# Top-64 attention: GpSimd lowers the scores below the 64th largest, ScalarE then takes exponentials and sums in place

## The reference, cut to what matters

```python
q, k = l2norm(q), l2norm(k)                        # k and v begin with 4 memory rows
dots = einsum('bhid,bhjd->bhij', q, k) * 10
dots = einsum('hg,bgij->bhij', W_pre_th, dots)     # heads are mixed
dots = where(causal, mask_value, dots)
# of each row only the 64 largest scores are kept
attn = softmax(dots)
attn = einsum('hg,bgij->bhij', W_post_th, attn)    # heads are mixed again
```

## Time and profile before

| | us |
|---|---|
| median of 3 runs | 4011.19 (4008.38 to 4012.89) |
| span of the profiled execution | 4014.9 |
| PE busy | 3618.5 (90%) |
| DVE busy | 3649.1 (91%) |
| ACT busy | 3158.1 (79%) |
| POOL busy | 723.3 (18%) |

### The profile page before, as it was taken

The page is one execution under the profiler, slowest core; times in us unless marked ns, Lnnn a source line. Parts: engine busy times, 40 slices in busy tenths (PEclk is TensorE's granted clock), DMA queues, the critical chain, the costliest instruction groups (busy, mean ns, idle before and its releaser), DMA issues. The chain is left out here.

```text
span 4014.9 us, 78409 instructions
## 1 busy us (share of the span) xinstructions
PE 3618.5 (90%) x19551; PEld 2620.4 (65%) x19551; DVE 3649.1 (91%) x19949; ACT 3158.1 (79%) x10004; POOL 723.3 (18%) x2487
## 2 busy tenths in 40 slices
PE   4999999986899999999999998999999999999987
PEld 3888888873566666666666666666666666666655
DVE  6888888845999999999999999999999999999995
ACT  5777777755788888888888888888888888888863
POOL 0000000002222222222222222222222222222221
PEclk8999999996999999999999999999999999999999
DMA  3000000001111111111111111111111111111110
GB/s 120 11 11 12 11 12 11 9 9 34 27 26 27 31 31 30 32 27 27 28 27 27 27 26 27 30 29 27 26 29 31 32 32 27 27 28 26 25 25 4
DMA packets 168119, 105.96 MB, mean 26 GB/s; under 512 B 78000, under 2 KB 165104, under 8 KB 166896
## 3 DMA queue, kind: packets, MB, share of 16 engines
q1 hardware_dynamic: 167664, 100.96, 11.8%
HBM read 20.70 MB, written 8.91 MB: 7 GB/s over the span
## 5 line engine op out<-in xcount | busy, mean ns | idle before, releaser
L1698 DVE MAX8 last<-W 128x8 f32<-128x130 f32 (+17 forms) x4032 | 944.2, 274 | 0.0
L1680 DVE MATCH_REPLACE8 W<-last,W 128x130 f32<-128x130 f32 (+17 forms) x3456 | 873.3, 259 | 0.0
L884 DVE TENSOR_TENSOR_SCAN hs<-dA,dx 128x256 f32<-128x256 f32 x512 | 351.2, 686 | 135.8 <-issue 100.7
L1789 POOL TENSOR_SCALAR posts<-post,share 128x128 f32<-128x128 f32 x1024 | 367.0, 376 | 513.0 <-DVE share L1612 510.1
L1487 ACT ACTIVATE SN<-bank,rq 128x260 f32<-128x260 f32 (+1 forms) x1024 | 361.3, 431 | 90.4 <-PE bank L1297 74.2
L1312 PE MATMUL bank<-T,pre 128*128 128x40 f32 (+15 forms) x1024 | 368.1, 442 | 62.5 <-DMA T<-SN 37.1
L1322 PE MATMUL bank<-posts,T 128*128 128x128 f32 (+7 forms) x2048 | 385.2, 291 | 3.6 <-POOL posts L1789 2.8
L1297 PE MATMUL bank<-kT,qT 64*128 64x260 f32 (+1 forms) x2048 | 275.1, 373 | 116.0 <-ACT SN L1487 108.3
L1322 PEld LDWEIGHTS bank<-posts,T 128*128 128x128 f32 (+7 forms) x2048 | 279.7, 170 | 94.3 <-issue 54.5
L1474 ACT ACTIVATE E<-T,peak 128x260 f32<-128x260 f32 (+12 forms) x800 | 305.3, 432 | 2.9
L1312 PEld LDWEIGHTS bank<-T,pre 128*128 128x128 f32 x1024 | 168.3, 195 | 206.4 <-ACT T L1495 95.2
(11 more groups left out here) (243 smaller groups left out, 8775.4 us busy)
## 6 DMA issues: line engine op xcount, KB each, us to landing
T<-SN SPq DMA_DIRECT2D x32, 130.0 KB
x_in<-in_xT SPq DMA_DIRECT2D x32, 128.0 KB, 2.3
x_mid<-x_b SPq DMA_DIRECT2D x32, 128.0 KB, 1.7
xb<-x_mid SPq DMA_DIRECT2D x32, 128.0 KB, 2.1
out_y<-x_d SPq DMA_DIRECT2D x32, 128.0 KB, 3.4
T<-SN SPq DMA_DIRECT2D x32, 126.0 KB
T<-SN SPq DMA_DIRECT2D x32, 122.0 KB
T<-SN SPq DMA_DIRECT2D x32, 118.0 KB
```

The costliest lines, as they stand in the source:

```text
L884: dve.tensor_tensor_scan(hs[j % NH][:], dA[j % ND][:], dx[b % 2][:], 0.0, ALU.mult, ALU.add).then_inc(scanned, 1)
L1680: dve.match_replace(both[:, s, at:to], best[n], both[:, s, at:to], LOWEST).then_inc(ranked, 1)
L1698: dve.max(best[n], both[:, s, at:to]).then_inc(ranked, 1)
L1789: pool.tensor_scalar(posts[(4 * k + j) % NP][:], post[:], share[k % 2][:, j:j + 1], 1.0, ALU.mult, ALU.mult).then_inc(posts_made, 1)
```

## The change

- `keep` and the tiles `E` are gone from DVE and ACT. DVE's rank ends with the MAX8 that finds the threshold; it raises `found_wide` or `found_narrow`.
- New on POOL: `drop(b, i)`, once for each quad. For each pair of groups that has something to cut (13 pairs in a block) it writes, group by group, -1e30 or 0 into the tile `below` (TENSOR_SCALAR, is_lt or is_gt with the threshold, then mult; a memset for group 6) and then adds the pair's `below` to the scores in `T` (TENSOR_TENSOR).
- ACT takes all 32 exponentials of a block in place in `T`, with the sum. It now waits for `dropped` (or, for whole pairs, for the mask).
- DVE's `rank` of quad k waits at its start for `dropped` of quad k-2 and `peaked` of quad k-2; for low groups that are not wide the TENSOR_REDUCE comes first. `turn_over` no longer waits for DVE's cuts; the new waits ahead of `wide` and `narrow` are on DVE's own earlier steps.
- ACT's table switches are made by `table(name)`, which loads a set only if another one is loaded; the `ACT_SET` beats are gone.
- All beats are new. DVE's rank still fills beats 16i to 16i+15.

```diff
-    E = [room.sb(f"E{j}", [P, KEYS if j < 2 else W_LO]) for j in range(4)]
+    below = [room.sb(f"below{n}", [P, 2 * (KEYS, W_LO)[n]]) for n in range(2)]
...
-    ACT_PEAK = (-2, 1, 34, 48, 64, 70, 81, 103)
-    ACT_WIDE = (-1, 20, 37, 50, 66, 70, 85, 103)
-    ACT_NARROW = (12, 30, 38, 50, 67, 73, 86, 114)
-    ACT_SET = (41, 52, 68, 79)
-    ACT_GATES = (47, 48, 50, 51)
-    ACT_SILU = (60, 61)
-    ACT_H1 = (70, 70)
-    ACT_H2 = (73, 74)
-    DVE_SHARE = (36, 38, 50, 65, 89, 98, 120, 130)
+    ACT_PEAK = (7, 10, 18, 52, 56, 63, 116, 131)
+    ACT_WIDE = (10, 12, 27, 54, 66, 83, 122, 131)
+    ACT_NARROW = (11, 17, 31, 56, 67, 102, 122, 131)
+    ACT_GATES = (31, 34, 43, 47)
+    ACT_SILU = (39, 41)
+    ACT_H1 = (60, 62)
+    ACT_H2 = (67, 75)
+    DVE_SHARE = (40, 51, 69, 85, 111, 111, 122, 136)
+    POOL_SHARE = (22, 30, 33, 47, 74, 87, 91, 121)
+    POOL_DROP = (-1, 21, 27, 30, 51, 61, 72, 101)
...
         def exps(b, i, pair):
             k = QUADS * b + i
+            table(EXP_LN)
             act.wait_ge(peaked, k + 1)
+            if k >= 4:
+                act.wait_ge(shared, k - 3)
+            if 2 * pair in DROPS[i]:
+                act.wait_ge(dropped, drops(k, 2 * pair))
+            else:
+                act.wait_ge(masked, HALF * b + PAIR_AT[QUAD[i][2 * pair]] + 1)
             for j in (2 * pair, 2 * pair + 1):
...
-                    act.activation(E[j][:, 0:n], scores(b, g), ACT.Exp, bias=least).then_inc(e_made, 1)
+                one = scores(b, QUAD[i][j])
+                act.activation(one, one, ACT.Exp, bias=peak[k % 2][:, j:j + 1], accum_out=total[k % 4][:, j:j + 1]).then_inc(e_made, 1)
...
-        def keep(b, i, j, best, base, op):
-
-            k, g = QUADS * b + i, QUAD[i][j]
-            dve.wait_ge(e_made, 4 * k + j + 1)
-            dve.scalar_tensor_tensor(out=scores(b, g), in0=base, scalar=best, in1=E[j][:, 0:width(g)], op0=op, op1=ALU.mult,
-                                     accum_out=total[k % 4][:, j:j + 1]).then_inc(cut_made, 1)
...
+        def drop(b, i):
+
+            nonlocal marks
+            k, made = QUADS * b + i, []
+            for j0 in DROPS[i]:
+                g = QUAD[i][j0]
+                w, x = width(g), side_by_side(b, g)
+                out = below[j0 // 2][:, 0:2 * w].rearrange("p (two n) -> p two n", two=2)
+                if drops(k, j0) > 1:
+                    pool.wait_ge(dropped, drops(k, DROPS[i][0]) - 1)
+                if g in WIDE:
+                    pool.wait_ge(found_wide, 2 * ((QUADS + 1) * b + i + j0 // 2 + 1))
+                else:
+                    pool.wait_ge(found_narrow, len(TURNED) * b + 1 + TURNED.index(QUAD[i][j0 + 1]))
+                for j in (j0, j0 + 1):
+                    one, best = QUAD[i][j], last8[k % 2][:, j, :]
+                    s, at = side(one), (seen_by(one) - TOPK) % 8
+                    if one in WIDE:
+                        pool.tensor_scalar(out[:, s, :], x[:, s, :], best[:, 7:8], DROP, ALU.is_lt, ALU.mult).then_inc(marked, 1)
+                    elif one in TURNED:
+                        pool.tensor_scalar(out[:, s, :], neg[2 * (i % 2) + one % 2][:, 0:w], best[:, at:at + 1], DROP, ALU.is_gt,
+                                           ALU.mult).then_inc(marked, 1)
+                    else:
+                        pool.memset(out[:, s, :], 0.0).then_inc(marked, 1)
+                marks += 2
+                made.append((x, out, marks))
+            for x, out, n in made:
+                pool.wait_ge(marked, n)
+                pool.tensor_tensor(x, x, out, ALU.add).then_inc(dropped, 1)
```

235 lines of the change are left out of this document (121 added, 114 removed).

## The result

The changed kernel takes 4057.51 us (median of 4 runs, 4057.01 to 4059.75) against 4012.04 for the kernel before on the same chip: the recorded ratio is 1.0104, with a 95% interval of 1.0092 to 1.0116 (the two medians alone give 1.0113). It is 1.0% slower. The prediction was 3876, faster, with a range up to 4030: wrong in sign and by 181 us.

What follows compares the result with a forecast made beforehand. DVE was taken to set the pace, PE next. Both at 86.5 us plus 3.5 of gaps gave 90.0 a block against 94.3: 138 us less over 32 blocks, 3 more in the drain, 3876 median; range 3800 to 4030.

Steps and rivals of the forecast that it cites:

- DVE, what is removed: Removing `keep` takes 8.8 us a block of busy time off DVE, from 92.3 to 83.5.
- I price them at nothing: DVE's new waits on its own earlier steps cost nothing, a few tenths of a us at most.
- POOL, what is added: The drops add 21 us a block on POOL, 10.3 compares and 10.6 adds; POOL goes from 22 to 43.
- the compare at the two-input slope, 26 us: Upper bound for POOL's added work a block, pricing compares by TENSOR_TENSOR's 1.9 ns a column.
- 0.4 to spare: Quad 7's chain from drop to share takes 4.6 us and fits in about 5 us of the next rank.
- The place of the drop: Behind quad 7's rank, the drop takes 3.0 us and four exponentials 1.6 before the share in the next block.
- ACT: Added accumulator reads cost up to 2.5 us a block, fewer table loads save 6.4: from 79.5 to about 75.6.
- The shared port: DVE's two-input operations lose 3.0 us a block beside POOL, between 0 and 11, putting DVE at 86.5.
- slower: the port: Rival: 18 opening TENSOR_TENSORs of DVE each wait a whole POOL instruction; 96.5 us a block, 4085 us; chance 0.14.
- PE: PE's work is unchanged, only its order changes: 86.5 us a block.
- The sum: DVE and PE both need 86.5 us; with 3.5 allowed for gaps, 90.0 a block, 4.3 less, over 32 blocks.
- The chain behind `drop` is late: Rival: late drops make DVE or PE wait, losing two to four us a block; 3947 to 4003 us; chance 0.19.

Runs made afterwards that it cites:

- the subtraction's run: The changed kernel with POOL's compare replaced by a subtraction, then a multiplication by 0, so nothing is dropped: 4042.6 us.
- filling: The changed kernel with matmuls of constants, result overwritten, in TensorE's gaps ahead of the first norm's spread and two premixes: 3996.5 us.
- the second version: Changed kernel with quads 6, 7 marked on DVE, quad 7's adds ahead of the mask, quad 4's posts ahead of drop 6: 4002.9 us; gaps filled, 3942.2.

## Why the prediction was wrong

Point by point, by its own steps.

- **DVE, what is removed.** Near: 85.0 us a block (forecast 83.5, with the port 86.5), by two errors that nearly cancel. `keep` gave 7.4 us and not 8.8, since its start and end run under its neighbours: the trace before, with L1618 taken out, is busy 84.9 us a block. The port cost 0.1 to 0.2 in place of 3.0. The step "I price them at nothing", of DVE's waits on its own steps, held; a new one on POOL's adds (L1728) takes 0.4 us a block.
- **POOL, what is added.** This is the step that failed: "25 x 0.27 + 4196 x 0.00083 = 10.3 us". It is 23.4. The slope was taken from multiplications; 21.2 of the 23.4 us are the compares with nothing of DVE's beside them, 2.2 what they lose beside DVE. The adds were right. The stated upper bound, "the compare at the two-input slope, 26 us", was one for compares and adds together (it makes the 48 of "29 to 48"), and it didn't hold either: the drops take 34.6 us and POOL 57.5. No row before the change had a compare on POOL, so neither of the two slopes was a bound. Nor was it carried on what even 26 would do to "0.4 to spare" for quad 7.
- **The place of the drop.** "For quad 7 it takes 3.0 us" was 5.3, and the drop began 2.9 us after the rank's end, behind the mask on POOL: 4.6 us of chain became 9.4. The queue was read for what stands behind the drops, not for what stands ahead.
- **ACT.** Right: 75.7 us, and 192 table loads, 6 a block.
- **The shared port.** DVE paid next to nothing; POOL did, by 0.39 to 0.50 us for each compare that starts beside the opening of a rank. The 0.11 us a piece was read from L1659 beside `neg` against L1688, another step; in the changed kernel L1674 of 180 columns, with nothing of POOL's beside it, takes 338, which leaves 0.08. The rival "slower: the port" gave the right sign by a mechanism that did not occur.
- **PE.** "86.5 us a block" was 87.4. The work was the same; the clock was lower. Missing from the prediction is that a gap of PE can cost twice, once as a wait and again as slower matmuls behind it; its clock was put at "0.99" for both kernels without a term.
- **The sum.** "I allow 3.5" for waits between two full engines; PE idles 8.4 us a block and DVE 10.9. Near the forecast's price of a drop (24.1 us a block for 21) and with the clock nearly held the kernel takes 3917.7, 1.3 us a block more than 3876: that is what the allowance missed. So, of the 181 us, 97 are the compare's price, 15 are those of the subtraction's run, of open cause, 28 are the clock at the low price, and 42 are left, by difference, for waits. The shares hang on the order in which they are taken: at the real price the clock alone is worth 61.
- **The rivals.** "The chain behind `drop` is late" was the right mechanism, mis-sized: 2 to 4 us a block lost were thought of, 5.8 came (95.8 - 90.0), the lower clock in it, and it was not let across the line to slower.

The Trainium skill ("SBUF — State Buffer", section "Who interferes with whom") has the shared port pair as an exclusive lock, held by whoever issues first. The trace agrees in part: POOL's instruction that starts beside DVE's pair loses time (0.8 us where 0.3 is usual at 2 columns), but DVE's L1701 of 180 columns, which starts under a running compare, takes 337 ns, as L1674 of that width does with nothing beside it (338), so it waits for no lock.

The Trainium skill ("TensorE: Matmul & The Clock Gate", section "HAM oscillation — how this bites in real kernels") charges a throttled stretch at half its length. By that the 5.3 us a block that filling took away (5.9 to 0.6) would be worth 2.7, an estimate of 85 us over 32 blocks; filling gave 61 here, and in the second version, where 10.1 us a block went, it gave 61 again for an estimate of 162, so the rule is an upper figure for this case.

What stays open: why the subtraction was 15 us faster than the compare at nearly the same price; how the 61 us of the filling divide between the spread and the premixes, which were filled together; and which waits make up the last 42 us.

## What to carry to other kernels

Price an instruction by rows with the same operation, not only with the same engine, width and operands: on POOL a compare of 180 columns took 0.89 us and a multiplication 0.41. A slope of another operation is no upper bound: here it said 26 us and 34.6 came. When a step goes on an in-order engine, look at what stands ahead of it too, and carry a price that no row shows through the tightest chain before giving the sign. When a change opens gaps on TensorE, count them as lost clock as well; a few matmuls of constants ahead of a known wait gave 1.5% here, about as much as moving marks to DVE and mending POOL's order together (1.3%).

## What the runs showed of the hardware

- POOL's TENSOR_SCALAR, with nothing of DVE's ranks beside it: at 132 columns 730 ns for is_lt against a per-partition operand and a multiplication, 661 with a constant, 621 for is_lt alone, 378 for two multiplications; a subtraction and a multiplication took 729. At 260 columns the first took 1.16 us and two multiplications 0.48.
- A TENSOR_SCALAR of POOL on 2 columns took 0.29 to 0.31 us, and up to 0.81 where it started beside two-input instructions of DVE. Compares of 148 to 260 columns lost 0.39 to 0.50 us so. DVE's instructions beside compares were not slowed (422 ns at 260 columns); one beside `posts` was (479 ns where 387 was usual).
- TensorE's granted clock fell to its lower level behind gaps of 1.2 to 2.4 us that stood among other idle time, for 3 to 10 us at a time; two premixes took 2.07 us in place of 1.13.
- Some versions with such gaps scattered by up to 1.3% (3980 to 4031), one by 0.2% once they were filled (1.2% before); the changed kernel itself has such gaps and scattered by 0.1%.
